# Chunk 0 of the feed-forward input rounded behind the scan, its stages re-ordered, the residual summed on TensorE

## The reference

```python
x = x + mamba4(layernorm(x))     # 4 layers: in_proj, conv, selective scan over 16 states, gate, out_proj
x = x + ffn(layernorm(x))
x = x + attention(layernorm(x))  # 16 heads of 8, causal, additive bias
x = x + ffn(layernorm(x))

def fp4_quant_dequant(x):        # blocks of 16 along the last dim
    scale = max(max(abs(block)) / 6, 1e-12)
    return GRID[searchsorted(MID, abs(block / scale))] * sign * scale   # grid 0 .5 1 1.5 2 3 4 6

def ffn(x):                      # width 352
    h = silu(q(x) @ q(w_gate).T) * (q(x) @ q(w_up).T)
    return q(h) @ q(w_down).T
```

## Time and profile before

| | |
|---|---|
| median of 3 runs | 1036.28 us (1035.46 to 1037.93) |
| the profiled execution | 1035.28 us, its span 1033.6 us |
| TensorE busy | 949.8 us (92%) |
| VectorE busy | 902.6 us (87%) |
| ScalarE busy | 761.5 us (74%) |
| GpSimd busy | 760.9 us (74%) |
| TensorE's mean granted clock | 0.97 |

### The profile page before, as it was taken

The page is one execution under the profiler, slowest core; times in us unless marked ns, Lnnn a source line. Parts: engine busy times, 40 slices in busy tenths (PEclk is TensorE's granted clock), DMA queues, the critical chain, the costliest instruction groups (busy, mean ns, idle before and its releaser), DMA issues. The chain is left out here.

```text
span 1033.6 us, 29750 instructions
## 1 busy us (share of the span) xinstructions
PE 949.8 (92%) x11909; PEld 580.2 (56%) x11909; DVE 902.6 (87%) x1724; ACT 761.5 (74%) x1683; POOL 760.9 (74%) x426
## 2 busy tenths in 40 slices
PE   5799999999999999999999999988477999999786
PEld 2455555565555555555555555655346566666456
DVE  6879998999989999899998999999699767787597
ACT  5888898988989889899898897984434255555442
POOL 1688999989999899999999989998254223333243
PEclk9799999999999999999999999999888999999888
DMA  6745453544535444454444544440571010000001
GB/s 187 254 160 166 137 173 125 166 147 162 167 128 164 147 165 146 145 167 146 165 146 138 158 147 159 147 132 14 128 155 21 21 23 17 7 2 2 1 0 41
DMA packets 69272, 120.88 MB, mean 117 GB/s; under 512 B 40072, under 2 KB 51152, under 8 KB 60112
## 3 DMA queue, kind: packets, MB, share of 16 engines
q1 hardware_dynamic: 69136, 118.98, 37.3%
HBM read 111.10 MB, written 6.29 MB: 114 GB/s over the span
## 5 line engine op out<-in xcount | busy, mean ns | idle before, releaser
L902 DVE TENSOR_TENSOR_SCAN hid<-decay,acc 128x256 f32<-128x256 f32 x1024 | 604.6, 664 | 40.9 <-PE acc L539 40.4
L1002 POOL TENSOR_TENSOR prod<-hid,c_rep 128x1024 f32<-128x1024 f32 x256 | 600.7, 2380 | 43.8 <-DVE hid L902 32.9
L765 ACT ACTIVATE decay<-delta,a_neg 128x255 f32<-128x255 f32 x1024 | 428.4, 502 | 47.6 <-DVE hid L902 47.4
L539 PE MATMUL acc<-b_diag,du_t 64*64 64x256 f32 x4096 | 273.1, 383 | 15.9 <-DVE hid L902 12.2
L567 PE MATMUL ring<-prod,ident 64*64 64x256 f32 x4096 | 255.5, 379 | 2.2 <-POOL prod L1002 2.2
L539 PEld LDWEIGHTS acc<-b_diag,du_t 64*64 64x64 f32 x4096 | 147.9, 134 | 124.8 <-DVE hid L902 55.3
L567 PEld LDWEIGHTS ring<-prod,ident 64*64 64x64 f32 x4096 | 152.0, 133 | 83.5 <-issue 22.7
L1916 POOL TENSOR_SCALAR_AFFINE_SELECT att_probs<-att_probs 128x512 f32<-128x512 f32 x64 | 41.1, 642 | 102.5 <-ACT att_probs L1959 100.1
L1959 ACT ACTIVATE att_probs<-acc 128x384 f32<-128x384 f32 x128 | 55.8, 488 | 52.5 <-PE acc L1733 52.5
L444 PE MATMUL ring<-xpad,diag_cw 64*64 64x512 f32 x512 | 60.5, 589 | 0.0
L1116 POOL TENSOR_TENSOR ffn_h_value<-ffn_h,ffn_h_inv 128x704 f32<-128x704 f32 x16 | 23.7, 1480 | 43.2 <-DVE ffn_h_value L1139 32.5
(11 more groups left out here) (180 smaller groups left out, 1263.7 us busy)
## 6 DMA issues: line engine op xcount, KB each, us to landing
c_rep<-c_rows SPq DMA_DIRECT2D x64, 1024.0 KB, 4.7
b_diag<-diag_rows SPq DMA_DIRECT2D x62, 512.0 KB, 3.9
diag_rows<-zeros SPq DMA_DIRECT2D x2, 2048.0 KB, 12.4
att_qk<-in_pos_q SPq DMA_DIRECT2D x4, 768.0 KB
att_qk<-in_pos_k SPq DMA_DIRECT2D x4, 768.0 KB
att_qk<-att_dense SPq DMA_DIRECT2D x24, 64.0 KB
resid<-in_x SPq DMA_DIRECT2D x4, 256.0 KB, 3.9
c_rows<-bc SPq DMA_DIRECT2D x64, 8.0 KB, 1.5
```

The lines of the kernel that those rows point to most:

```text
L539: last = nc.tensor.matmul(inj[m * HALF:(m + 1) * HALF, K % 2, at:at + HALF * SG], du_t[rows, n % 2, e, chans:chans + HALF], b_diag[rows, K ...
L765: last = nc.scalar.activation(decay[:, K % DECAYS, s, 1:], delta[:, n % 2, h, e * SEQ + 1:(e + 1) * SEQ], ACT.Exp, scale=a_neg[:, lay(n) % ...
L902: last = nc.vector.tensor_tensor_scan(hid[:, K % HIDS, s, :], decay[:, K % DECAYS, s, :], rows[:, s, :], 0.0, ALU.mult, ALU.add)
L1002: nc.gpsimd.tensor_tensor(prod[:, K // 2 % PRODS, h], hid[:, K % HIDS, :, :], c_rep[:, g, :, at], ALU.mult).then_inc(s_prod, 1)
```

## The change

1. `Inputs` of ffn1 exist from the start. In the scan's last turn VectorE takes the moments of chunks 0 and 1 behind groups 6 and 12 and an offset behind group 9, ScalarE an rstd in group 8. Behind the last group VectorE does chunk 0's scales, its normalisation to the scale (`vector_normal`, formerly on GpSimd), exponent and rounding, and chunk 2's moments, all ahead of `gating`; GpSimd dequantises chunk 0.
2. The rounded x takes the place of `core.normed`; the tile `xq` and the x rounder's `value` are gone.
3. In `ffn_stage` `early` is 1 for ffn1 and 3 for ffn2. The lags are one turn shorter: `turn_h` two turns and `down` three behind. Gate and down have one PSUM bank each. The transposes of x and of h share a bank. The rounding step of h (`held`) is one PSUM region of two banks, so ScalarE writes it to PSUM and a step waits for the rounding before it.
4. `add` is gone. `down` begins each tile's sum with the product of the identity and `core.resid` (four more instructions for two tiles), and ScalarE copies the sum back (`copy_down`).
5. The table load of the silu stands ahead of `copy_x(0)`, chunk 3's normalisation behind `gate(0)`.
6. Attention's strips of groups 2 and 3, its first values and GpSimd's four setting instructions move from attention's block into the end of ffn1. Group 0 and 1 swap their PSUM banks.

The diff, cut to its core:

```diff
@@ scan, ScalarE
+                        if k == 8 and not more:
+                            norm.scalar_rstd(a, 0)
...
+                norm.scalar_normalise(a, 0)
+                norm.scalar_rstd(a, 1)
+                first.q.scalar_step(a, 0)
+                norm.scalar_normalise(a, 1)
+                norm.scalar_rstd(a, 2)
+                norm.scalar_normalise(a, 2)
@@ scan, VectorE
+                        if n == NPAIR - 1:
+                            if k in (6, 12):
+                                chunk_moments(k // 6 - 1)
+                            if k == 9:
+                                norm.vector_offset(v, 0)
+                first.vector_scales(v, 0)
+                first.vector_normal(v, 0)
+                first.q.vector_exponent(v, 0)
+                norm.vector_offset(v, 1)
+                chunk_moments(2)
+                first.q.vector_round(v, 0)
                 gating(NPAIR - 1)
+                norm.vector_offset(v, 2)
                 add_out(NPAIR - 1)
@@ scan, GpSimd
+                first.pool_dequant(p, 0)
@@ ffn_stage, banks
-        gate_bank = [bank(ring, 1), bank(ring, 2)]
-        up_bank = [bank(ring, 3), bank(acc, 0)]
-        hT_bank = [bank(acc, 1)[:, 0:2 * P], bank(acc, 1)[:, 2 * P:4 * P], bank(acc, 2)[:, 0:2 * P]]
-        down_bank = [bank(acc, 3)[:, 0:2 * P], bank(ring, 0)[:, 0:2 * P]]
+        qh = Rounder(core, sb, "h", HCOLS // BLK, 4, acc[:, 2 * BANK:2 * BANK + HCOLS])
+        x_bank, gate_bank, up_bank = bank(ring, 0), bank(ring, 1), [bank(ring, 2), bank(acc, 0)]
+        hT_bank = [bank(ring, 0)[:, 0:2 * P], bank(ring, 0)[:, 2 * P:4 * P], bank(acc, 1)[:, 0:2 * P]]
+        down_bank = bank(ring, 3)[:, 0:2 * P]
@@ ffn_stage, VectorE
+                for k in range(HSTEPS + 1):
+                    if k >= 2:
+                        qh.vector_exponent(v, k - 1)
+                    if k == 2:
+                        x.q.vector_exponent(v, 3)
+                    if attention and k == HSTEPS - 1:
+                        v.wait_ge(s_add, 2)
+                        attention.norm.vector_moments(v, 0)
                     if k < HSTEPS:
                         hidden(k)
+                    if k == 0 and early == 1:
+                        x.q.vector_round(v, 1)
+                        x.q.vector_exponent(v, 2)
+                    if k == 1:
+                        qh.vector_exponent(v, 0)
                         x.vector_scales(v, 3)
+                    if attention and k == HSTEPS:
                         attention.norm.vector_normalise(v, 0)
+                    if k >= 1:
+                        qh.vector_round(v, k - 1)
+                    if k == 1 and early == 1:
+                        x.q.vector_round(v, 2)
+                    if k == 2:
+                        x.q.vector_round(v, 3)
@@ ffn_stage, TensorE
-                        need(t, s_silu, n - 1)
+                        need(t, s_silu, n)
...
+                    need(t, s_add, k)
                     for i in range(2):
+                        at = down_bank[:, i * P:(i + 1) * P]
+                        nc.tensor.matmul(at, ident[:, :], core.resid[:, 2 * k + i, :], start=True, stop=False)
@@ ffn_stage, ScalarE
+                def copy_down(k):
+                    a.wait_ge(s_down, k + 1)
+                    nc.scalar.activation(resid_flat[:, k * 2 * P:(k + 1) * 2 * P], down_bank, ACT.Copy).then_inc(s_add, 1)
...
+                norm.scalar_rstd(a, 3)
+                nc.scalar.preload_act_table_set(SILU)
+                copy_x(0)
+                if early == 1:
                     x.q.scalar_step(a, 1)
                 gate(0)
+                norm.scalar_normalise(a, 3)
+                for k in range(HSTEPS + 2):
                     if 1 <= k <= HSTEPS:
                         qh.scalar_step(a, k - 1)
+                    if k == 0 and early == 1:
+                        x.q.scalar_step(a, 2)
+                    if k == 2:
+                        x.q.scalar_step(a, 3)
                     if k + 1 < HSTEPS:
                         gate(k + 1)
...
+                    if k in (0, 2, 4):
                         copy_x(k // 2 + 1)
+                    if k >= 2:
+                        copy_h(k - 2)
                     if k >= 3:
+                        copy_down(k - 3)
```

More of the change, by code:

```diff
@@ L223, in mamba_stage @@
     y = core.ring[:, 0:2 * BANK]
-    core.minus_step = core.sb("minus_step", [P, 1])
+    norm = first.norm
     with ExitStack() as stage:
@@ L1085, in __init__ @@
         self.inv = sb(f"{tag}_inv", [P, depth, blocks])
-        self.value = sb(f"{tag}_value", [P, depth, blocks * BLK])
+        self.values = values or [self.value_tile(sb, tag, n) for n in range(depth)]
         self.step = sb(f"{tag}_step", [P, depth, blocks * BLK])
@@ L1129, in scalar_step @@
         a.wait_ge(self.s_exponent, c + 1)
-        self.core.nc.scalar.activation(self.step[:, i, :], self.step[:, i, :], ACT.Relu, bias=self.core.minus_step[:, :],
+        if self.held is not None and c:
+            self.s_round.wait(a, "rounded", c - 1)
+        self.core.nc.scalar.activation(self.steps(i), self.step[:, i, :], ACT.Relu, bias=self.core.minus_step[:, :],
                                        scale=HALF_STEP).then_inc(self.s_step, 1)
@@ L1152, in __init__ @@
         self.core, self.norm = core, norm
-        self.q = Rounder(core, sb, "x", CH // BLK)
-        self.xq = sb("xq", [P, CHUNKS, CH])
         self.normed = core.normed[:, :, :].rearrange("p t (b k) -> p (t b) k", k=BLK)
+        rows = core.normed[:, :, :].rearrange("p t d -> p (t d)")
+        self.q = Rounder(core, sb, "x", CH // BLK, values=[rows[:, c * CH:(c + 1) * CH] for c in range(CHUNKS)])
     def blocks(self, c):
@@ L1411, in _ @@
                     attention.wait(t)
-                    t.wait_ge(s_silu, 2 * HSTEPS)
-                    t.wait_ge(s_xTc, CHUNKS)
+                    t.wait_ge(s_hTc, HSTEPS)
+                    qh.s_round.wait(t, "rounded", HSTEPS - 1)
                     attention.tensor_strips(t, 0)
                     t.wait_ge(s_add, HSTEPS)
-                    attention.tensor_strips(t, 1)
+                    for g in range(1, HGROUPS):
+                        attention.tensor_strips(t, g)
+                    attention.tensor_values(t, 0)
             @block.scalar
@@ L1800, in project_out @@
                     banks.fill(last, "proj", b)
-                for g in range(2, HGROUPS):
-                    tiles.tensor_strips(t, g)
-                project_v(0)
                 t.wait_ge(s_maskb, 2)
@@ L1870, in add_out @@
                     banks.read(nc.vector.tensor_tensor(at, at, banks.bank("proj", b)[:, 0:SEQ], ALU.add), "proj", b)
-                for g in range(2, HGROUPS):
-                    tiles.vector_strips(v, g)
-                values(0)
                 v.wait_ge(s_npk, 1)
```

257 lines of the change are left out of this document (111 added, 146 removed).

## The result

The changed kernel takes 1055.65 us (median of 4 runs, 1050.55 to 1060.67) beside 1035.87 for the kernel before: ratio 1.0193, 95% interval 1.0165 to 1.0221. It is 20 us slower; the forecast said 2 us slower, with 1042.0 as the upper end. The profiled execution took 1056.19 us, its span 1054.5 (before 1035.28 and 1033.6), and TensorE's mean granted clock is 0.955 (0.97 before).

What follows compares the result with a forecast made beforehand. VectorE was taken to bound the kernel now, TensorE most later feed-forward steps. Seven stretches, +4.9 - 5.5 + 7.5 - 4.2 + 1.0 + 2.7 - 4.6, gave +1.8 us: span 1035.4, median 1038.1, range 1031.5 to 1042.0.

Steps and rivals of the forecast that it cites:

- F: Second feed-forward stage, `hidden` 0 to `hidden` 7: 40.5 us where it was 37.8, costing 2.7.
- C: First feed-forward stage, `hidden` 0 to `hidden` 7: 50.0 us where it was 42.3, costing 7.5.
- rival 2: Slower by TensorE's half clock in the drains, 2.8 to 4 us more for both stages: 1041.5 us; chance 0.19.
- A: Scan's tail: costs 4.9 us, the first feed-forward block starting at 733.0 instead of 728.1.
- The x scale's 1.9 us: Behind the last scan: chunk 0's scale instruction waits for GpSimd's last product and takes some 1.9 us.
- B: First feed-forward block's start to its first `hidden`: 7.0 us where it was 12.5, giving back 5.5.
- D: First stage's `hidden` 7 to attention's first peak: 25.9 us where it was 30.0, giving back 4.2.
- E: Head of the second feed-forward stage: its first `hidden` comes 1.0 us later.
- G: Second stage's `hidden` 7 to the end of the span: 17.7 us where it was 22.3, giving back 4.6.
- VectorE's step of 4.85: Feed-forward stages: VectorE's own work per two tiles, 5.69 us less 0.33 for the residual's addition and 0.51 of waiting.
- 1: Rival: VectorE, not TensorE, keeps setting the pace at 4.85 us a step, -5.4: 1032.7; chance 0.27 including an earlier head.
- 3: Rival: the rounding with its step in PSUM still waits for GpSimd, step 5.9 us, +0.4 in 12 steps: 1043; chance 0.08.

Runs made afterwards that it cites:

- after_warm_again: The changed kernel with unread products filling TensorE's waits in the feed-forward stages; ratio 1.0091 to the kernel before.
- gating_first: The changed kernel with the scan's last gating ahead of chunk 2's moments and chunk 0's rounding; ratio 1.0187 to the kernel before.
- after_warm_orders: after_warm_again plus the order of gating_first and ScalarE's rounding step of chunk 2 behind step 1's silus; ratio 1.0084 to the kernel before.
- two_gate: The changed kernel with h's rounding step back in SBUF and a freed bank as second gate bank; ratio 1.0215 to the kernel before.

## Why the prediction was wrong

**F, and the later half of C: the step that failed.** The forecast put TensorE's steady loop at full clock ("gate and up of tile one (0.59 apart, ...), then an idle 0.7 for the silu (0.46) with its handoffs, gate and up 1.18") and asked for the half clock only behind long idle times, in the drains (rival 2). It never asked what the 0.55 at each tile, and the longer waits at a stage's head, do to the clock. Measured: 0.50 from 742 to 772 us and from 976 to 994 (then 0.55 to 0.69 until 1012). F from `hidden` 0 to the scales of step 1 took 12.1 us for 8.8 in the sum (three tiles at 3.3), its last four steps 24.7 for 21.5, of which 1.4 are x's transposes (below) and the rest is mostly clock (22.9 in `after_warm_again`). With the clock nearly full the two stretches give C 50.6 and F 42.2, within 0.6 and 1.7 of the forecast: the arithmetic described the kernel at 2.4 GHz. That C comes so near is in part luck, as too much clock loss in its first half stands against too small terms in its second. The clock moved 3.8 us in C and 5.6 in F, 9.4 of the 19.1 missed, and 11 in the medians.

**What was right in C.** `hidden` 3 stands 28.2 us behind `hidden` 0 (27.4 forecast), since there half clock and ScalarE's queue were in the sum (25.6 in `after_warm_again`, where the clock was held); the loop without x is 5.63 (5.5). Two terms were too small: x's transposes add 1.4 to a step, not 0.5, because they share a bank with h's, and h's then wait 0.78 for the copy; and attention's moments, 1.2, stand ahead of `hidden` 7 on VectorE (C's last step is 6.83). The other 1.6 us of C's last four steps lie in the first two (6.2 each): their gate and up products ran at half clock until 776 us. In `after_warm_again` the four take 25.0 in place of 26.3.

**A.** Three parts: the offset among the scans collided with GpSimd (1.03 for 0.1), and behind chunk 1's moments the scans waited 0.23 for TensorE; the out products, 2.02 in the kernel before, took 3.60 at half clock, a price that the forecast did not put beside its 2.4; and some 0.5 is the scan itself, whose end differs by 3 to 4 us between profiles of kernels with the same scan. The out products' half clock followed an idle time of 3.67 for the later gating (1.44 before). That this idle time is the reason is not shown: in `gating_first` it is 1.42, and the out products still took 3.72, the clock having fallen to 0.50 by 726 us, under the sum of states. The x scale's 1.9 us was right. Two slips of 0.2 in the recorded sum (2.5 + 4.7 written as 7.0, 50.0 - 42.3 as 7.5) change nothing.

**B, D, E, G** hold within 0.2, 0.8, 0.1 and 1.7 us. The shorter pipeline gives back 6.3 of the 8.8 us that were forecast; round 7 ended 8.7 us behind `hidden` 7 (8.9).

**VectorE's step of 4.85** is real only where the collision is gone: with the step in PSUM and the clock full VectorE takes 4.84 (1002.18 to 1007.02 in `after_warm_again`). In the kernel before, taking the addition away gives nothing, so the subtraction of 0.33 from the earlier trace rows was wrong for that kernel: the scale's wait takes its place.

**Rivals.** 1 did not happen (VectorE idles 0.7 to 2.1 a step). 3 did not either (0.89 beside GpSimd). 2 had the right cause at the wrong place: it put the half clock into the drains, but it is the start of each stage that loses the clock. It was priced at 3 to 4 us, and filling took back 11.

**Still open:** what in the remaining 9 us of `after_warm_again` is the one bank, what the scan's tail and attention's 1 to 2 us; on the kernel before, one bank alone leaves as much (1.0092), but giving the changed kernel its second gate bank gained nothing in the total. The single down bank and the bank that x's and h's transposes share were not tried apart. That the 1.5 us at the border make the clock fall is argued from where it falls, and not tested.

## What to carry to other kernels

A PSUM bank that is handed from TensorE to ScalarE and back at each tile can cost twice, by the wait and by the clock that the waits keep down (20 us in the kernel before, 11 of them the clock); before a bank is spent on something else, price the loop at both clock levels and read from the trace which one a stretch with such waits is granted. A microsecond taken off the busiest engine counts only if nothing behind it waits for another engine's fixed end; look whether an instruction just behind has a duration longer than its shortest. Where TensorE's share is high but its products take twice their shortest duration, adding unread products is a cheap experiment that separates clock from order.

## What the runs showed of the hardware that was not expected

- With waits of 0.55 us at a tile, and some of 0.7 and 3.4, TensorE stayed at a granted clock of 0.50 for 30 us (742 to 772). With unread products in the waits it was at 1.00 there but for one window of 0.72 (`after_warm_again`).
- A fall of the clock outlasts its cause: behind 1.5 us of idle time it stayed at 0.50 for 38 us with TensorE busy all the time (`after_warm_orders`; 20 us in `two_gate`), in some kernels' profiles and not in others with the same idle time. It cost 7 to 17 us there. One kernel's times spread over 10 to 20 us; that this is the reason in the executions without a profile is likely, not shown.
- An instruction of VectorE on 4 columns that meets GpSimd takes 1.03 us in place of 0.15, and 32 columns 1.86 in place of 0.18 (the changed kernel, 706.75 and 723.84).
